# Deformable sampling: the running sums leave PSUM's chain of products and are added in SBUF by GpSimd

## The chip, the cores and the metric

The kernel runs on one core of a Trainium2 chip. The metric is the device time of one launch in microseconds (us). Shapes are written as partitions x elements per partition.

## What is computed

A block of convolution with attention: a deformable convolution (DCNv3) on a 4 x 56 x 56 x 128 image, an attention layer over all rows, and a mixture of experts. The change lies in the deformable sampling alone:

```python
B, H, W, C, G = (4, 56, 56, 128, 16); K = 9; GC = C // G
px = gx + dx + off[..., 0]
py = gy + dy + off[..., 1]
x0 = jnp.floor(pxf); y0 = jnp.floor(pyf)
for cx, cy in ((x0, y0), (x0 + 1, y0), (x0, y0 + 1), (x0 + 1, y0 + 1)):
    wgt = (1 - jnp.abs(pxf - cx)) * (1 - jnp.abs(pyf - cy))
    v = jnp.take_along_axis(xg, idx, axis=1)
    acc = acc + (wgt * valid)[..., None] * v
out = (acc * mf).reshape(B, H * W, K, G, GC).sum(axis=2)
```

Each pixel has 16 groups of 8 channels, and each group samples the projected image at 9 places of its own, bilinearly, with softmax weights over the 9.

## The kernel before

The program is a row of stages with a barrier of all engines between them: offsets and masks (about 80 to 700 us), a table of windows (to 741 us), the sampling (741 to 2215 us), the rest of the block over rows (to about 2515 us), attention, and the experts.

**The sampling stage** (`deformable_stage`, which calls `window_pass`) replaces the gather by arithmetic. The 128 partitions are 128 tiles of 7 x 14 pixels. The work is cut in 32 units: 16 channel groups (g) by two halves (v) of a tile, 49 pixels each. For a unit, every tap's bilinear weight is written as a product of two "hat" functions of row and column, and the weights of the nine taps are added into one grid `wd` of 8 x 8 shifts around each pixel. The unit's output is then the sum over these 64 shifts of weight times shifted image.

- SyncE loads the offsets (`om`) and the window of the image (`xw`) of the next group, 32 DMAs a group.
- ScalarE (`hats`, `clear`) computes the hat functions and zeroes `wd`, one unit ahead; `finish` (L714 to L720) moves a finished unit out of PSUM.
- VectorE (`build_step`) adds up the next unit's grid (L768, L774, L785, L792), and between these steps makes the current unit's products (`apply`, L832): 16 instructions of 4 shifts, 128x1568 elements, in a ring of four buffers `prod`.
- TensorE (L736 to L749) adds the products up in PSUM: an identity matrix times each 392-column quarter of a product, 64 matmuls a unit, into one of two accumulators `acc[:, v]`. In float32 each matmul is two records of the profile.
- GpSimd has nothing to do in this stage.

What has already been summed for these output elements lies in `y_all` (128 x 98 x 128 in SBUF, zeroed in an earlier stage at L252), since the pass can run for several windows of positions; with these inputs it runs once. Before a unit's products, one more matmul puts the old sums into the accumulator (L743), and `finish` copies the accumulator back over them (L717):

```python
pe.matmul(out, ident[:, :], unit_y(g, v), start=True, stop=False)      # L743
nc.scalar.activation(unit_y(g, v), acc[:, v, 0:UPX * GC]..., ACT.Copy)  # L717
```

`unit_y` (L676) is the unit's part of `y_all`: 7 rows of 7 pixels of 8 channels, 392 elements in runs of 8 with a step of 128. What orders the work: `prod_ok` and `prod_used` between VectorE and TensorE (VectorE is at most four products ahead), `acc_free` from `finish` to TensorE, `hats_ok` and `blank` from ScalarE to VectorE, `dstep` between VectorE's own steps. `hold` (L86) waits and then raises a semaphore of its own. After the pass GpSimd clears the semaphores (L886), and VectorE steps the window (L889 to L893).

Of the kernel before, what the change touches and what calls it, by code (L numbers as in the profile page):

```python
# [7 lines left out]
ALU = mybir.AluOpType  # L8
ACT = mybir.ActivationFunctionType
# [5 lines left out]
G, K = 16, 9  # L15
GC = C // G
# [11 lines left out]
R = 4  # L28
GRID = 8
OFFMAX = 58.0  # L30
LANES = 128
NB8, NXB = 8, 4
BY, BX = H // NB8, W // NXB
PX = BY * BX
UX = BX // 2
UPX = BY * UX
# [49 lines left out]
def hold(eng, sem, value, own):  # L86

    eng.wait_ge(sem, value)
    eng.sem_inc(own, 1)
# [508 lines left out]
NPROD = 4  # L598
# [37 lines left out]
def window_pass(nc, k, tb, bufs, sems, xg_d, om_d, y_all):  # L636

    own, ident = k["own"], k["ident"]
    om, xw, hat, mk, wd, prod, zeros, acc, ad = bufs
    (om_in, x_in, rel_ok, abs_ok, hats_ok, blank, hym_ok, dstep, prod_ok, prod_used, acc_free, y_ok) = sems  # L640
    DVE, SP = mybir.EngineType.DVE, mybir.EngineType.SP
    NCHUNK = 2 * GRID
    why = "an offset within the grid of positions, clamped when the table was made"
# [1 line left out]
    with nc.Block() as block:  # L645
# [30 lines left out]
        def unit_y(g, v):  # L676

            y = y_all[:, :, :].rearrange("p (y x) c -> p y x c", x=BX)
            return y[:, :, v * UX:(v + 1) * UX, bass.ds(g * GC, GC)]

        @block.scalar
        def _(act):
            act.sem_inc(acc_free, 2)

            def hats(g, v):
                n = g * 2 + v
                h = hat[:, v, :, :, :]
                if v == 0:
                    hold(act, om_in, g * 256 + 256, own)
                for s in range(2 * K):  # L690
                    d, tap = s // K, s % K
                    last = nc.scalar.activation(  # L692
                        h[:, s, R - 1, :].rearrange("p (y x) -> p y x", x=UX),
                        om[:, g % 2, :, v * UX:(v + 1) * UX, s], ACT.Identity,
                        bias=tb["nsk"][:, :, :, :].rearrange("p g d k -> p (g d k)")[:, bass.ds(g * (2 * K) + s, 1)],
                        scale=1.0)
                last.then_inc(rel_ok, 1)
                nc.scalar.activation(mk[:, v, :, :].rearrange("p k (y x) -> p k y x", x=UX),
                                     om[:, g % 2, :, v * UX:(v + 1) * UX, 2 * K:POS].rearrange("p y x k -> p k y x"),
                                     ACT.Copy)  # L700
                hold(act, rel_ok, n + 1, own)
                for r in range(R):
                    last = nc.scalar.activation(h[:, :, r, :], h[:, :, R - 1, :], ACT.Abs, bias=tb["negr"][:, r:r + 1],
                                                scale=1.0)
                last.then_inc(abs_ok, 1)
                hold(act, abs_ok, n + 1, own)
                flat = h.rearrange("p s r q -> p (s r q)")
                nc.scalar.activation(flat, flat, ACT.Relu, bias=1.0, scale=-1.0).then_inc(hats_ok, 1)

            def clear(v):  # L710
                nc.scalar.activation(wd[:, v, 0:GRID * WROW], zeros[:, 0:1].to_broadcast([LANES, GRID * WROW]), ACT.Copy)\  # L711
                    .then_inc(blank, 1)

            def finish(g, v):  # L714
                n = g * 2 + v
                hold(act, prod_used, n * NCHUNK + (NCHUNK + NPROD), own)
                nc.scalar.activation(unit_y(g, v), acc[:, v, 0:UPX * GC].rearrange("p (y x c) -> p y x c", y=BY, x=UX),  # L717
                                     ACT.Copy).then_inc(y_ok, 1)
                hold(act, y_ok, n + 1, own)
                act.sem_inc(acc_free, 1)  # L720

            for v in range(2):
                hats(0, v)
                clear(v)
            with act.Fori(0, G - 1) as g:
                for v in range(2):
                    n = g * 2 + v
                    hold(act, dstep, (n + 1) * PER, own)
                    hats(g + 1, v)
                    hold(act, prod_ok, (n + 1) * NCHUNK, own)  # L730
                    clear(v)
                    finish(g, v)
            for v in range(2):
                finish(G - 1, v)

        @block.tensor  # L736
        def _(pe):
            with pe.Fori(0, G) as g:
                for v in range(2):
                    n = g * 2 + v  # L740
                    hold(pe, acc_free, n + 1, own)
                    out = acc[:, v, 0:UPX * GC]
                    pe.matmul(out, ident[:, :], unit_y(g, v), start=True, stop=False)  # L743
                    for s in range(NCHUNK):
                        pe.wait_ge(prod_ok, n * NCHUNK + (s + 1))
                        for i in range(NXH):
                            mm = pe.matmul(out, ident[:, :], prod[:, s % NPROD, i, :], start=False,  # L747
                                           stop=(s == NCHUNK - 1 and i == NXH - 1))
                        mm.then_inc(prod_used, 1)  # L749

# [100 lines left out]
def deformable_stage(nc, k, tb, xg_d, om_d, y_all):  # L851

    with ExitStack() as es:
        t = Ctx(nc, es, "deform")
        names = ("om_loaded x_loaded rel_ready abs_ready hats_ready grid_blank hym_ready dve_step prod_ready prod_used "
                 "acc_free y_ready").split()
        sems = [t.sem(s) for s in names]
        tstep = t.sem("table_step")
        tmp = {"sr": t.sb("sr", [LANES, G, 2, K]), "wf": t.sb("wf", [1, G, K]), "pc": t.sb("pc", [1, G, 2]),
               "xf": t.sb("xf", [1, G])}  # L860
        zeros = t.sb("zeros", [LANES, 1])
        bufs = (t.sb("om", [LANES, 2, BY, BX, POS]), t.sb("xw", [LANES, 2, LANE_ROWS, LANE_COLS]),
                t.sb("hat", [LANES, 2, 2 * K, R, UPX]), t.sb("mk", [LANES, 2, K, UPX]),
                t.sb("wd", [LANES, 2, GRID * WROW + R * UPX]),
                t.sb("prod", [LANES, NPROD, NXH, UPX * GC]), zeros, t.ps("acc", [LANES, 2, 512]),
                t.sb("ad", [LANES, 4, R, R * UPX]))

        def move(body):
            with nc.Block() as block:
                @block.vector  # L870
                def _(dve):
                    body(dve)

        def restart(dve):
            nc.vector.memset(zeros[:, :], 0.0)
            nc.vector.tensor_copy(tb["p0"][:, :, :], tb["base"][:, :, :])

        move(restart)
        why = "a count of windows, bounded by the clamp of the offsets"
        nx, ny = (nc.values_load(tb["counts"][0:1, i:i + 1], min_val=1, max_val=int(2 * OFFMAX + 6) // R + 1,  # L880
                                 skip_runtime_bounds_check_because=why) for i in range(2))
        with nc.Fori(0, ny) as iy:
            with nc.Fori(0, nx) as ix:
                pass_tables(nc, tb, tmp, tstep)
                window_pass(nc, k, tb, bufs, sems, xg_d, om_d, y_all)
                for s in sems + [tstep, k["own"]]:  # L886
                    nc.gpsimd.sem_clear(s)
                nc.all_engine_barrier()
                move(lambda dve: nc.vector.tensor_scalar(tb["p0"][:, :, 0], tb["p0"][:, :, 0], tb["step"][:, 0:1], None,  # L889
                                                         ALU.add))  # L890
            move(lambda dve: nc.vector.tensor_scalar(tb["p0"][:, :, 1], tb["p0"][:, :, 1], tb["step"][:, 1:2], None,
                                                     ALU.add))
            move(lambda dve: nc.vector.tensor_copy(tb["p0"][:, :, 0], tb["base"][:, :, 0]))  # L893
# [1394 lines left out]
```

## Time and profile before

| | |
|---|---|
| median of 3 timed runs | 4370.42 us (4362.55, 4370.42, 4370.85) |
| the profiled execution: its time | 4365.95 us |
| the profiled execution: its span | 4364.2 us |
| TensorE busy, whole span | 3101.0 us (71%) |
| VectorE busy, whole span | 3029.8 us (69%) |
| ScalarE busy, whole span | 1418.7 us (33%) |
| GpSimd busy, whole span | 686.7 us (16%) |

The busy shares are means over stages that have different limits; what bounds the sampling is to be read from that stage. The time of an execution holds 1.75 us more than its span. In the profile PE is TensorE's matmuls, PEld its weight loads, DVE VectorE, ACT ScalarE, POOL GpSimd, SP SyncE; a q behind a name is that engine's instruction queue. Records of matmuls overlap, since they are pipelined: their pitch, from start to start, tells more than their length.

### The profile page before, as it was taken

To read this page: it belongs to the slowest core of one execution; us is meant where nothing else is said; L and a number is where in the kernel's file an instruction comes from. 1 tells how busy PE (TensorE), PEld (TensorE's weight loads), DVE (VectorE), ACT (ScalarE), POOL (GpSimd) and SP (SyncE) were. 2 spreads that over 40 slices of the span, in tenths; PEclk is the share of its full clock that TensorE was granted. 3 is DMA by queue.
4 is the path that set the end of the run, shared out by engine and by line. 5 is a ranking of instruction groups with operands and counts; after the bars stand their busy time and mean duration, and the time that the engine had idled before them with its cause. 6 is when DMAs were issued, how large, how long until landed. Compare 5 with 4: busy or idle time off the path is not lost. (4 is left out here: it accounts for less than half of the span.)

```text
span 4364.2 us, 40182 instructions
## 1 busy us (share of the span) xinstructions
PE 3101.0 (71%) x10947; PEld 1781.1 (41%) x10947; DVE 3029.8 (69%) x4442; ACT 1418.7 (33%) x2562; POOL 686.7 (16%) x724
## 2 busy tenths in 40 slices
PE   0144432799999999999965559999999996308940
PEld 0022221455555555555543324454544444306630
DVE  0387875899999999999969946666666664400026
ACT  0022221543333434242111145536455440103332
POOL 1033221000000000000035500111111111360036
PEclk9967666899999999999977679999999995559975
DMA  7732213222121212121021110010010102002223
GB/s 168 182 80 52 51 49 75 43 29 29 24 35 24 34 23 33 27 34 24 0 66 48 47 52 1 1 45 1 17 28 1 30 1 84 6 25 80 82 61 87
DMA packets 210585, 193.86 MB, mean 44 GB/s; under 512 B 65997, under 2 KB 181597, under 8 KB 210016
## 3 DMA queue, kind: packets, MB, share of 16 engines
q1 hardware_dynamic: 171506, 141.42, 15.3%
q10 hardware_dynamic: 32686, 42.09, 4.0%
q0 software_dynamic: 6272, 8.99, 1.1%
q8 instruction: 45, 0.74, 0.1%
q14 instruction: 76, 0.62, 0.0%
HBM read 94.01 MB, written 102.30 MB: 45 GB/s over the span
## 5 line engine op out<-in xcount | busy, mean ns | idle before, releaser
L747 PE MATMUL deform_acc<-deform_prod,all_ident 128*128 128x392 f32 x4096 | 1379.9, 495 | 74.3 <-DVE deform_prod L832 69.0
L747 PEld LDWEIGHTS deform_acc<-deform_prod,all_ident 128*128 128x128 f32 x4096 | 769.5, 190 | 680.1 <-DVE deform_prod L832 173.0
L832 DVE TENSOR_TENSOR deform_prod<-deform_xw,deform_wd 128x1568 f32<-128x1568 f32 x512 | 910.3, 1789 | 19.3 <-DVE deform_wd L792 10.8
L1494 PE MATMUL attn_ps_r<-attn_prob,attn_xs 128*128 128x448 f32 (+1 forms) x1400 | 607.6, 563 | 64.4 <-DVE attn_xr L1710 57.0
L1591 ACT ACTIVATE attn_prob<-attn_ps_e,attn_nm 128x896 f32<-128x896 f32 (+3 forms) x400 | 364.8, 913 | 469.8 <-DVE attn_nm L1679 467.9
L1679 DVE TENSOR_REDUCE attn_nm<-attn_ps_e 128x1 f32<-128x896 f32 (+3 forms) x400 | 385.4, 970 | 163.6 <-PE attn_ps_e L1482 152.7
L1494 PEld LDWEIGHTS attn_ps_r<-attn_prob,attn_xs 128*128 128x128 f32 (+1 forms) x1400 | 256.3, 194 | 313.7 <-issue 188.2
L711 ACT ACTIVATE deform_wd<-deform_zeros 128x3136 f32<-128x3136 f32 x32 | 90.1, 2815 | 805.9 <-DVE deform_prod L832 805.9
L2141 DVE TENSOR_TENSOR experts_yo<-experts_ps_y,experts_b 128x512 f32<-128x512 f32 x32 | 22.1, 691 | 394.3 <-PE experts_ps_y L2081 394.3
L1710 DVE TENSOR_TENSOR attn_xr<-attn_xr,attn_ps_r 128x448 f32<-128x448 f32 x252 | 155.7, 618 | 160.1 <-PE attn_ps_r L1494 157.5
L792 DVE TENSOR_TENSOR deform_wd<-deform_wd,deform_ad 128x784 f32 x256 | 249.4, 974 | 1.0 <-DVE deform_wd L792 0.5
L985 POOL MEMSET rows_half<- 128x4 f32 x1 | 0.1, 101 | 1519.5 <-POOLq L67 1519.5
L1391 POOL TENSOR_TENSOR attn_xs<-attn_xa,attn_wz 128x508 f32<-128x508 f32 (+1 forms) x100 | 100.7, 1032 | 863.1 <-DVE attn_wz L1700 863.1
L785 DVE TENSOR_TENSOR deform_ad<-deform_hat 128x1568 f32<-128x1568 f32 x128 | 228.8, 1788 | 0.0
L1482 PE MATMUL attn_ps_e<-attn_ka,attn_qa 128*128 128x448 bf16 (+1 forms) x700 | 200.9, 357 | 9.4 <-DVE attn_qb L1672 5.6
L1482 PE MATMUL attn_ps_e<-attn_kb,attn_qb 128*128 128x448 bf16 (+1 forms) x700 | 200.0, 356 | 0.0
L692 ACT ACTIVATE deform_hat<-deform_om,block_nsk 128x49 f32 (+1 forms) x576 | 162.8, 375 | 97.4 <-DMA deform_om<-offsets_masks 74.4
L301 PE MATMUL offs_ps_x<-all_ident,offs_x_sb 112*128 112x112 f32 x112 | 26.1, 385 | 193.9 <-ACT offs_xt L356 181.8
L292 PE MATMUL offs_ps_c<-all_ident,offs_conv 128*112 128x128 f32 x112 | 21.4, 324 | 190.6 <-DVEq L468 129.0
L2111 ACT ACTIVATE experts_hid<-experts_ps_u,experts_b1t 128x512 f32<-128x512 f32 x128 | 87.8, 687 | 163.7 <-PE experts_ps_u L2070 163.6
L2081 PE MATMUL experts_ps_y<-experts_w,experts_hid 128*128 128x128 f32 x1024 | 121.9, 277 | 23.0 <-ACT experts_hid L2111 23.0
L460 DVE TENSOR_SCALAR offs_conv<-offs_xpad,block_w_dw,block_b_dw_col 128x1568 f32<-128x1568 f32 x8 | 8.4, 1092 | 184.3 <-ACT offs_xt L356 184.3
(299 smaller groups left out, 4118.4 us busy)
## 6 DMA issues: line engine op xcount, KB each, us to landing
offsets_masks<-offs_om SPq DMA_DIRECT2D x56, 378.0 KB
deform_om<-offsets_masks SPq DMA_DIRECT2D x256, 82.7 KB
deform_xw<-projected SPq DMA_DIRECT2D x256, 73.5 KB
projected<-offs_zero ACTq DMA_DIRECT2D x1, 17000.0 KB
dispatched<-offs_zero ACTq DMA_DIRECT2D x1, 8192.0 KB
experts_bi<-dispatched SPq DMA_DIRECT2D x32, 256.0 KB, 3.3
expert_out<-experts_yo ACTq DMA_DIRECT2D x32, 256.0 KB, 3.8
projected<-offs_zero ACTq DMA_DIRECT2D x1, 7480.0 KB
```

The lines of the kernel that those rows point to most:

```text
L692: last = nc.scalar.activation(h[:, s, R - 1, :].rearrange("p (y x) -> p y x", x=UX), om[:, g % 2, :, v * UX:(v + 1) * UX, s], ACT.Identity ...
L747: mm = pe.matmul(out, ident[:, :], prod[:, s % NPROD, i, :], start=False, stop=(s == NCHUNK - 1 and i == NXH - 1))
L785: nc.vector.tensor_tensor(dst, spread(hat[:, v, tap:tap + 2, :, :], 2, R), spread(hat[:, v, K + tap:K + tap + 2, :, :], 3, R), ALU.mult).t ...
L792: nc.vector.tensor_tensor(region, region, temp(tap), ALU.add).then_inc(dstep, 1)
L832: nc.vector.tensor_tensor(prod[:, s % NPROD, :, :].rearrange("p d (y x c) -> p d y x c", y=BY, x=UX), x, spread(w.rearrange("p (d y x) -> ...
L1391: pool.tensor_tensor(xs[0:rows, at + i, :, 0:C - 1], spread(xa[0:rows, b % 2, tile, 0:C - 1], 1, NCH), spread(wz[0:rows, e, i, :], 2, C - ...
L1482: mm = pe.matmul(ps_e[u % NE][0:rows, hf, 0:BK], q_[:, S % 2, at:at + rows], k_[:, b % 2, m0:m0 + BK], start=q_ is qa, stop=q_ is qb)
L1494: mm = pe.matmul(ps_r[:, 0:BK], xs[0:rows, at + i, j // 2, :], prob[0:rows, at + i, j * BK:(j + 1) * BK], start=(i == 0), stop=(i == len(t ...
L1591: nc.scalar.activation(prob[0:rows, slab(S) + i, m0:m0 + n * BK].rearrange("p (a f) -> p a f", a=n), ps_e[u % NE][0:rows, 0:n, 0:BK], ACT. ...
L1679: nc.vector.tensor_reduce(nm[0:rows, S % 2, i, ch:ch + 1], ps_e[u % NE][0:rows, 0:halves(ch), 0:BK], mybir.AxisListType.XY, ALU.max, negat ...
L1710: nc.vector.tensor_tensor(part, part, ps_r[:, 0:BK], ALU.add).then_inc(r_ok, 1)
L2081: mm = pe.matmul(ps_y[p][:, j * C:(j + 1) * C], hid[:, p, f, j * 128:(j + 1) * 128], w2[:, x, f, :], start=(f == 0), stop=(f == FB - 1))
```

## The change

The matmul that puts the old sums into the accumulator is gone; the first product's matmul starts the accumulator instead. `finish` copies the accumulator to a new buffer `sums` (128 x 2 x 392, one part for each half v), and GpSimd, with a block of its own in the pass, adds that buffer to the unit's part of `y_all`, in place. A new semaphore `added` tells ScalarE that the half's buffer may be written again; it starts at 2. One more semaphore is cleared at the end of the pass.

```diff
         @block.scalar
         def _(act):
-            act.sem_inc(acc_free, 2)
-
...
             def finish(g, v):
                 n = g * 2 + v
                 hold(act, prod_used, n * NCHUNK + (NCHUNK + NPROD), own)
-                nc.scalar.activation(unit_y(g, v), acc[:, v, 0:UPX * GC].rearrange("p (y x c) -> p y x c", y=BY, x=UX),
-                                     ACT.Copy).then_inc(y_ok, 1)
+                hold(act, added, n + 1, own)
+                nc.scalar.activation(sums[:, v, :], acc[:, v, 0:UPX * GC], ACT.Copy).then_inc(y_ok, 1)
                 hold(act, y_ok, n + 1, own)
                 act.sem_inc(acc_free, 1)
 
+            act.sem_inc(acc_free, 2)
...
+        @block.gpsimd
+        def _(pool):
+            pool.sem_inc(added, 2)
+            with pool.Fori(0, G) as g:
+                for v in range(2):
+                    n = g * 2 + v
+                    hold(pool, y_ok, n + 1, own)
+                    part = unit_y(g, v)
+                    pool.tensor_tensor(part, part, sums[:, v, :].rearrange("p (y x c) -> p y x c", y=BY, x=UX),
+                                       ALU.add).then_inc(added, 1)
+
         @block.tensor
...
                     out = acc[:, v, 0:UPX * GC]
-                    pe.matmul(out, ident[:, :], unit_y(g, v), start=True, stop=False)
                     for s in range(NCHUNK):
                         pe.wait_ge(prod_ok, n * NCHUNK + (s + 1))
                         for i in range(NXH):
-                            mm = pe.matmul(out, ident[:, :], prod[:, s % NPROD, i, :], start=False,
+                            mm = pe.matmul(out, ident[:, :], prod[:, s % NPROD, i, :], start=(s == 0 and i == 0),
                                            stop=(s == NCHUNK - 1 and i == NXH - 1))
```

## Rows read from the trace of the kernel before

**Rows 1.** The page, part 2: tenths of busy time in 40 slices of 109 us

```profile
DVE  0387875899999999999969946666666664400026
POOL 1033221000000000000035500111111111360036
```

**Rows 2.** Windows, 800 to 2160 us: stretch, length, busy us (instructions), PEclk, DMA, GB/s

```profile
800.00:2160.00 1360.00, 1337.25 (x3993) 748.54 (x3992) 1349.09 (x921) 483.83 (x773) 0.00 (x0) 1.00 0.20 27
```

**Rows 3.** Waits, 800 to 2160 us: us in total, times, longest

```profile
PEld deform_acc L747 <- DVE deform_prod L832: 119.1, 236, 1.1
PE deform_acc L747 <- DVE deform_prod L832: 17.6, 44, 0.5
DVE deform_prod L832 <- DVE deform_wd L792: 10.4, 28, 0.4
DVE deform_prod L832 <- PE deform_acc L747: 0.3, 1, 0.3
```

**Rows 4.** Timeline, from the first product to a unit's border: start, us, work

```profile
792.69 3.49 DVE L832 TENSOR_TENSOR deform_prod<-deform_xw,deform_wd 128x1568 f32<-128x1568 f32 x2 [0.39 <-DVE deform_wd L792]
...
1193.37 0.52 PEld L743 LDWEIGHTS deform_acc<-block_y_all,all_ident 128*128 128x128 f32 x2
1194.08 0.50 ACT L717 ACTIVATE block_y_all<-deform_acc 128x392 f32 x1 [0.32 <-PE deform_acc L747]
1195.45 1.99 DVE L768 TENSOR_TENSOR deform_hat<-deform_hat,deform_mk 128x1764 f32<-128x1764 f32 x1
1197.36 1.78 DVE L832 TENSOR_TENSOR deform_prod<-deform_xw,deform_wd 128x1568 f32<-128x1568 f32 x1
```

**Rows 5.** Timeline, the last unit and the end of the stage

```profile
2167.84 10.30 DVE L832 TENSOR_TENSOR deform_prod<-deform_xw,deform_wd 128x1568 f32<-128x1568 f32 x6
2169.69 0.82 PE L743 MATMUL deform_acc<-block_y_all,all_ident 128*128 x2
2170.34 42.30 PE L747 MATMUL deform_acc<-deform_prod,all_ident 128*128 128x392 f32 x128
2178.45 1.79 DVE L832 TENSOR_TENSOR deform_prod<-deform_xw,deform_wd 128x1568 f32<-128x1568 f32 x1 [0.30 <-PE deform_acc L747]
2212.77 0.50 ACT L717 ACTIVATE block_y_all<-deform_acc 128x392 f32<-128x392 f32 x1 [42.30 <-PE deform_acc L747]
2214.97 0.23 DVE L889 TENSOR_SCALAR block_p<-block_p,block_step 128x16 f32<-128x16 f32 x1 [11.03 <-PEq L888]
```

**Rows 6.** Groups by form, GpSimd: xcount, busy us, mean ns, idle before

```profile
L1391 POOL TENSOR_TENSOR attn_xs<-attn_xa,attn_wz 128x508 f32<-128x508 f32 x96 | 96.8, 1032 | 863.1 <-DVE attn_wz L1700 863.1
L268 POOL TENSOR_TENSOR offs_om<-offs_om,offs_mx x28 | 33.5, 1196 | 43.1 <-DVE offs_mx L449 42.6
L1402 POOL TENSOR_TENSOR attn_tin<-attn_tin,attn_xa 128x512 f32<-128x512 f32 x24 | 30.3, 1266 | 120.2 <-DMA attn_tin<-block_out 120.2
L1402 POOL TENSOR_TENSOR attn_tin<-attn_tin,attn_xa 64x128 f32<-64x128 f32 x4 | 1.8, 447 | 1.0 <-DMA attn_tin<-block_out 1.0
```

**Rows 7.** Timeline of DVE and POOL in the rows stage; last row: L1095's min/median/max ns

```profile
2246.80 0.69 DVE L1101 TENSOR_TENSOR rows_z<-rows_z,rows_gg 128x512 f32<-128x512 f32 x1
2246.92 1.69 POOL L994 TENSOR_TENSOR rows_x_all<-rows_x_all,rows_gb 128x512 f32<-128x512 f32 x1
2247.41 1.79 DVE L1095 TENSOR_SCALAR rows_z<-rows_z,rows_mv,rows_rs 128x128 f32<-128x128 f32 x3
...
L1095 DVE TENSOR_SCALAR rows_z<-rows_z,rows_mv,rows_rs x196: 302/334/1295, 2230.9 to 2508.1; 128x128 f32<-128x128 f32 x196
```

**Rows 8.** Timeline of DVE and POOL, offsets stage, two places; last row: L259's min/median/max ns

```profile
234.46 1.36 DVE L438 SCALAR_TENSOR_TENSOR first_extremes<-offs_om,first_extremes 112x1152 f32<-112x1152 f32 x1
234.61 1.29 POOL L259 TENSOR_SCALAR offs_ve<-offs_mv 112x4 f32<-112x4 f32 x1 [0.47 <-DVE offs_mv L400]
...
278.28 1.32 POOL L274 TENSOR_TENSOR offs_om<-offs_om,offs_mx  x1 [4.36 <-DVE offs_mx L428]
278.90 1.92 DVE L438 SCALAR_TENSOR_TENSOR first_extremes<-offs_om,first_extremes 112x1152 f32<-112x1152 f32 x1 [0.34 <-DVE offs_om L430]
...
L259 POOL TENSOR_SCALAR offs_ve<-offs_mv x28: 222/1298/1316, 206.4 to 671.3; 112x4 f32<-112x4 f32 x28
```

More of the change, by code:

```diff
@@ L638, in window_pass @@
     own, ident = k["own"], k["ident"]
-    om, xw, hat, mk, wd, prod, zeros, acc, ad = bufs
-    (om_in, x_in, rel_ok, abs_ok, hats_ok, blank, hym_ok, dstep, prod_ok, prod_used, acc_free, y_ok) = sems
+    om, xw, hat, mk, wd, prod, zeros, acc, ad, sums = bufs
+    (om_in, x_in, rel_ok, abs_ok, hats_ok, blank, hym_ok, dstep, prod_ok, prod_used, acc_free, y_ok, added) = sems
     DVE, SP = mybir.EngineType.DVE, mybir.EngineType.SP
@@ L855, in deformable_stage @@
         names = ("om_loaded x_loaded rel_ready abs_ready hats_ready grid_blank hym_ready dve_step prod_ready prod_used "
-                 "acc_free y_ready").split()
+                 "acc_free y_ready added").split()
         sems = [t.sem(s) for s in names]
@@ L865, in deformable_stage @@
                 t.sb("prod", [LANES, NPROD, NXH, UPX * GC]), zeros, t.ps("acc", [LANES, 2, 512]),
-                t.sb("ad", [LANES, 4, R, R * UPX]))
+                t.sb("ad", [LANES, 4, R, R * UPX]), t.sb("sums", [LANES, 2, UPX * GC]))
         def move(body):
```

## The prediction

> **What bounds the kernel now.** I read the slices of the page first, then the windows, the waits and the timeline of the one stage that the change touches. The slices show VectorE at nine tenths or more from about 800 to 2160 us, with GpSimd at zero [rows 1]. In that stretch of 1360 us VectorE is busy 1349.1 us (99.2%), TensorE 1337.3 us, at a granted clock of 1.00 throughout [rows 2]. Both look full, and the waits tell them apart: TensorE and its weight loads wait for VectorE's products again and again (119.1 us in 236 waits, 17.6 us in 44), while VectorE waited for TensorE once, for 0.3 us. What is left of VectorE's idle time is a step of its own, 0.4 us at the head of a unit [rows 3]. So the sampling goes at VectorE's pace. From the first product of unit 0 (792.69) to that of unit 31 (2167.84) are 31 units, 44.36 us each [rows 4, 5]. Only the last unit is different: VectorE has no next grid to build, it waits for free buffers from 2178.45 on, and TensorE sets the end: 128 records in 42.30 us, a pitch of 0.33 us [rows 5].
>
> **What the change removes.** One float32 matmul a unit (L743), two records, which take TensorE 0.65 us from start to the next unit's first product matmul (2169.69 to 2170.34) [rows 5]. Over 32 units that is 21 us of TensorE's time. In the units 0 to 30 it buys nothing, because TensorE then only waits longer for VectorE, whose waits for it sum to 0.3 us [rows 3]. In the last unit it is on the path: **-0.65 us**.
>
> **What it adds on ScalarE.** The same copy of 392 elements (0.50 us, L717 [rows 4]), now to contiguous SBUF, and one more wait, for the add of two units earlier, some 88 us back. Nothing: ScalarE is busy 483.8 of the 1360 us [rows 2], and TensorE gets its accumulator back a unit early. If that wait ever did hold, the hats of a later unit would be queued behind it, and VectorE would wait for them.
>
> **What it adds on GpSimd: 32 adds.** First their length. Two inputs that are both full, as here, took 1266 ns for 512 elements and 447 ns for 128 [rows 6]: 2.13 ns an element and 0.17 us beside it, so 392 elements are **1.01 us**. Where one input repeats along the inner run it is cheaper, 1032 ns for 508 and 1196 ns for 576 elements [rows 6], which scaled to 392 is 0.80 us: my low end. L268 works on runs of 9 elements of 27 and is not slow; runs of 8 with a step of 128, as in `y_all`, no row shows.
>
> **What an add does to VectorE.** This is the term that decides, and GpSimd's idleness hides nothing of it, since VectorE has no gap of 1 us in the stage. Two places of the trace show the two engines getting into each other's way, in both directions:
>
> - GpSimd waits for VectorE. L259 works on 4 elements a partition and takes 222 ns at best, but 1.3 us when it starts beside L438, which has two inputs in SBUF: it ends at 235.90, just after L438 (235.82) [rows 8]. In the rows stage L994, an add of 512 elements like L1402, takes 1.69 us instead of 1.27 since L1101 is under way at its start [rows 7].
> - Then VectorE waits for GpSimd. The first L1095 behind L1101 takes up to 1295 ns instead of the median 334, because L994 runs till 2248.61: **0.96 us lost to an add of 1.27 us** [rows 7]. And L438, with two SBUF inputs like every VectorE instruction of the sampling (products, grid steps, mask), took 1.92 instead of 1.36 us where L274 still had 0.70 us to run: 0.56 us lost [rows 8].
>
> Both also show that the waiting GpSimd instruction gets in at the end of the VectorE instruction that held it, ahead of VectorE's next one. In the sampling stage VectorE runs one after another without a gap, so each add starts beside a product or a mask step (at 1194.6 it would be a product, with L768 next [rows 4]), waits for its end, and delays the next one. The size, from an add of 1.01 us: by L1095 the loss is the add's length less 0.31 us, 0.70 us. By L438, 0.14 us of what remained was no loss, another 0.14 us of GpSimd's record lies ahead of its need (L259 ends 0.08 us after L438 though it lasts 0.22 alone), and consecutive VectorE records overlap by 0.09 us, which is given up too: 1.01 - 0.28 + 0.09 = 0.82 us. I take the mean, **0.76 us**. The low end is the cheap add by the first rule, 0.80 - 0.31 = 0.49 us; the high end for a normal add 0.82 us.
>
> How often: the add of unit n falls at the head of unit n+1. For n = 0 to 29 that unit is bound by VectorE: 30 x 0.76 = **+22.8 us** (30 x 0.49 = 14.7 to 30 x 0.82 = 24.6). TensorE does not soften it; it only idles longer. The add of unit 30 falls into the last unit, where VectorE later idles for TensorE [rows 5]: nothing.
>
> The Trainium skill speaks against the change more sharply: "SBUF — State Buffer", section "Who interferes with whom", says that a VectorE instruction with two SBUF inputs and a GpSimd instruction that reads SBUF exclude each other for the whole instruction, whoever comes first. With a whole instruction lost each time the sum would be 30 x 1.01 = 30.3 us; the rows show the exclusion, but a loss some 0.2 to 0.3 us shorter, and I go by them.
>
> **The end of the stage.** The last add has no cover. Before, ScalarE's last copy ended at 2213.27 and the step of the window came at 2214.97 [rows 5]; now GpSimd's 1.01 us and some 0.2 us of semaphores lie between: **+1.2 us**. One semaphore more to clear: under 0.1 us, inside this. The other stages are the same.
>
> **Sum.** -0.65 + 22.8 + 1.2 = **+23.4 us** on the profiled execution's 4365.95 us, 4389.4. That execution is 4.5 us below the median shown; the four times of this kernel average 4367.4. I set the forecast between the sums on both, at **4391 us**.
>
> **The rivals.** A measurement of this kernel can tell 0.2% from no change, 8.7 us.
>
> - *No price (same).* GpSimd never gets in between VectorE's back-to-back instructions, or reads in VectorE's gaps (0.4 us at the head of a unit [rows 3]), and has 88 us for its 1 us. For it: in rows 7 the instruction that was overtaken has one tensor input, and the one overtaken behind L259 lost next to nothing to so small an operation. Against it: L438 itself lost 0.56 us. Time: 4366 to 4371 plus 0.55, about **4369**. Chance 0.11.
> - *Slow add (slower by more).* The 8-element runs of `y_all`, read and written, cost GpSimd twice the time, 2.0 us. Loss 2.0 - 0.25 = 1.75 us a unit, 30 times: +52 us, **4420**. Against it: L268's runs of 9 [rows 6]. Chance 0.07.
> - *TensorE is the bound (faster).* Place: the head of each unit, where it works off a backlog of products with L743 in front. If the 98% of rows 2 were a real limit, the removed 0.65 us would shorten each of 32 units: -21 us, **4347**, provided that the adds cost VectorE less than that. It decides only from the point at which VectorE waits for free product buffers; rows 3 have one such wait of 0.3 us. Chance 0.05.
>
> **How the numbers follow.** The forecast's case has the rest, 0.77. Its own ends are 14.7 + 0.55 on 4365.95, which is 4381, and 24.6 + 0.55 on 4370.4, which is 4396. To leave out no more than 2 in 10, the range takes in a somewhat slower add (1.3 us, a loss of about 1.0 us, +31) and 2 us of spread below: **4379 to 4402**. Slower by over 0.2%: 0.77 + 0.07, less the edge of the low end, 0.83; within 0.2%: 0.12; faster: 0.05.
>
> **What would show it.** In the profile after: VectorE's records no longer have the same length; once a unit a product or mask step (L768, L832) is 0.7 to 0.8 us longer than its 1.99 or 1.79 us; the pitch of the units is 45.1 instead of 44.36 us. GpSimd's adds last 1.0 us plus the wait for the instruction under way, up to 2.7 us, and 1.0 us for the last. VectorE's busy share stays at 99%, as the loss lies inside its records; TensorE's waits for products grow by about 1.4 us a unit. At the end L889 follows ScalarE's last copy by 2.9 instead of 1.7 us. I am wrong if the pitch stays at 44.4 (no exclusion between these forms), if an uncovered add lasts 2 us, or if TensorE's granted clock falls below 1.00 with its added idle time.

## The result, and the profile after

The changed kernel takes **4395.21 us** (median of 5, 4389.88 to 4401.05) where the kernel before takes 4370.42 us (median of 5, 4362.55 to 4375.50). The ratio is 1.0058, with a 95% interval of 1.0046 to 1.0071: slower by 0.6%, 24.8 us between the medians. The forecast was 4391 us, with 4379 to 4402 as its range. The profiled execution took 4389.88 us, with a span of 4388.1 us, 23.9 us more than before.

The same views as before, of the changed kernel. First the slices of the page and the windows view of 800 to 2160 us (busy us of PE, PEld, DVE, ACT, POOL, then PEclk, the DMA's share and GB/s):

```profile
DVE  0387874999999999999969946666666664400026
POOL 1033221000000000000025501010111111360036
...
800.00:2160.00 1360.00, 1309.20 (x3859) 717.56 (x3858) 1349.10 (x904) 484.38 (x775) 47.75 (x30) 1.00 0.20 27
```

VectorE's busy time is the same to a hundredth of a per cent, 1349.1 us, but it holds 904 instructions instead of 921 [rows 2]. A busy share says nothing of work done. GpSimd's 30 adds do not show in the slices at all: 47.75 us in 1360 is less than a tenth. TensorE's granted clock is 1.00 in this stretch, as before. The waits of the same stretch:

```profile
PEld deform_acc L756 <- DVE deform_prod L841: 192.2, 321, 1.2
PE deform_acc L756 <- DVE deform_prod L841: 45.9, 88, 0.6
DVE deform_prod L841 <- DVE deform_wd L801: 10.8, 29, 0.4
```

TensorE waits longer for VectorE (119.1 and 17.6 us before [rows 3]), and VectorE no longer waits for TensorE here at all. So the bound is what it was, and has become slower. Where, shows the view of single lines (min/median/max ns, first and last start in us); GpSimd's add is now L743, the mask step L777, the product L841:

```profile
L743 POOL TENSOR_TENSOR block_y_all<-block_y_all,deform_sums x32: 1001/1590/1660, 842.3 to 2240.0; 128x392 f32 x32
L777 DVE TENSOR_TENSOR deform_hat<-deform_hat,deform_mk x32: 1987/2810/2831, 774.8 to 2153.2; 128x1764 f32<-128x1764 f32 x32
L841 DVE TENSOR_TENSOR deform_prod<-deform_xw,deform_wd x512: 1772/1778/2606, 794.8 to 2228.5; 128x1568 f32<-128x1568 f32 x171
```

The mask step took 1.99 us in every unit; now it takes 2.80 to 2.83 us in the 30 units in front of which an add falls (median of all 32: 2.81). No other VectorE instruction of the sampling became longer, but for one product of the last unit (2606 ns). The timeline at one border between units shows how it comes about:

```profile
1202.82 0.50 ACT L716 ACTIVATE deform_sums<-deform_acc 128x392 f32<-128x392 f32 x1 [0.32 <-PE deform_acc L756]
1203.58 1.58 POOL L743 TENSOR_TENSOR block_y_all<-block_y_all,deform_sums 128x392 f32 x1 [43.59 <-ACT deform_sums L716]
1204.19 2.82 DVE L777 TENSOR_TENSOR deform_hat<-deform_hat,deform_mk 128x1764 f32<-128x1764 f32 x1
```

The add starts while a product is under way, waits for its end (about 1204.28, since records overlap by 0.09 us), works until 1205.16, and the mask step behind the product ends 0.83 us late. ScalarE's copy comes at the same point of every unit, so in this kernel it is always the mask step that pays. And the end of the stage (last unit's first products, last copy, last add, step of the window):

```profile
794.81 3.49 DVE L841 TENSOR_TENSOR deform_prod<-deform_xw,deform_wd 128x1568 f32<-128x1568 f32 x2 [0.39 <-DVE deform_wd L801]
...
2194.79 14.53 DVE L841 TENSOR_TENSOR deform_prod<-deform_xw,deform_wd 128x1568 f32<-128x1568 f32 x8
2197.78 1.38 POOL L743 TENSOR_TENSOR block_y_all<-block_y_all,deform_sums 128x392 f32 x1 [43.60 <-ACT deform_sums L716]
2239.25 0.50 ACT L716 ACTIVATE deform_sums<-deform_acc 128x392 f32<-128x392 f32 x1 [41.74 <-PE deform_acc L756]
2240.01 1.00 POOL L743 TENSOR_TENSOR block_y_all<-block_y_all,deform_sums 128x392 f32 x1 [40.85 <-ACT deform_sums L716]
2242.67 0.23 DVE L898 TENSOR_SCALAR block_p<-block_p,block_step 128x16 f32<-128x16 f32 x1 [12.34 <-PEq L897]
```

From unit 0's first product to unit 31's are now 1399.98 us, before 1375.15 [rows 4, 5]: +24.8. From there to the step of the window are 47.88 us, before 47.13: +0.75. Together 25.6 us. The span grew by less than that, 23.9 us; the difference lies in stages that the change does not touch: unit 0's first product comes 2.1 us later, and what follows the sampling is 3.8 us shorter. In the experiments below the first product lies anywhere from 794 to 800 us, also where nothing ahead of it differs from the kernel before, so such differences are from run to run. Below I therefore read the **pitch of the units** (first product to first product, mean over the 28 units from unit 1 on): 44.375 us before, 45.204 after.

### The profile page after: what moved, and what is told of

Read it like the earlier page. It is cut to its first block and busy times, and to the rows that moved or that the text cites. A ratio compares the mean times of both kernels' runs of the same rounds, so it can differ in the third digit from the quotient of the medians.

```text
span 4388.1 us, 40187 instructions
## 1 busy us (share of the span) xinstructions
PE 3085.1 (70%) x10883; PEld 1756.7 (40%) x10883; DVE 3055.9 (70%) x4442; ACT 1419.4 (32%) x2562; POOL 736.6 (17%) x756
## 5 line engine op out<-in xcount | busy, mean ns | idle before, releaser
L841 DVE TENSOR_TENSOR deform_prod<-deform_xw,deform_wd 128x1568 f32<-128x1568 f32 x512 | 906.3, 1781 | 18.1 <-DVE deform_wd L801 11.2
L743 POOL TENSOR_TENSOR block_y_all<-block_y_all,deform_sums 128x392 f32 x32 | 50.1, 1567 | 1494.7 <-ACT deform_sums L716 1494.7
```

Source lines behind the costliest of these rows:

```text
L841: nc.vector.tensor_tensor(prod[:, s % NPROD, :, :].rearrange("p d (y x c) -> p d y x c", y=BY, x=UX), x, spread(w.rearrange("p (d y x) -> ...
```

## The experiments

Theory 1: GpSimd's add and a VectorE instruction with two inputs in SBUF exclude each other while they read; the removed matmul was worth nothing outside the last unit. The rivals are named in each expectation. Reference times of the kernel before on the same chips: medians 4368.65 to 4369.26 us (13 runs each); the changed kernel was not timed again beside them. Where an experiment has one run, its time says little, since runs of one kernel lie up to 18 us apart, and the argument rests on the pitch and on the records of its trace. The edits are shown against the changed kernel, except in "No add at all" and "The add on VectorE", which start from the kernel before; `...` stands for lines left out.

**No add at all.** The kernel before, less the matmul:

```diff
-                    pe.matmul(out, ident[:, :], unit_y(g, v), start=True, stop=False)
...
-                            mm = pe.matmul(out, ident[:, :], prod[:, s % NPROD, i, :], start=False,
+                            mm = pe.matmul(out, ident[:, :], prod[:, s % NPROD, i, :], start=(s == 0 and i == 0),
```

> The kernel before without the matmul that reads the old sums into PSUM, and with no add at all: ScalarE writes each finished unit straight over its part of y_all. It leaves out the summing over several windows. Theory 1 (the add and VectorE exclude each other; the matmul was free): the pitch of the units stays at 44.36 us as before, and only the last unit is shorter, by 0.65 us, so the time is that of the kernel before within its spread. Rival (TensorE is a real limit of each unit): the pitch falls by up to 0.65 us a unit, 20 us in all.

Measured: 4370.19 us against 4368.65, ratio 1.000 (0.9990 to 1.0009). The pitch is 44.378 us. Its last unit, by its first products and the step of the window:

```profile
2175.58 12.00 DVE L831 TENSOR_TENSOR deform_prod<-deform_xw,deform_wd 128x1568 f32<-128x1568 f32 x7
2219.96 0.50 ACT L717 ACTIVATE block_y_all<-deform_acc 128x392 f32<-128x392 f32 x1 [41.74 <-PE deform_acc L746]
2222.16 0.23 DVE L888 TENSOR_SCALAR block_p<-block_p,block_step 128x16 f32<-128x16 f32 x1 [11.03 <-PEq L887]
```

46.58 us instead of 47.13, so 0.55 us gained, once. TensorE was no limit of the other units, though it is busy for 98% of the stretch in the kernel before.

**Matmul and add together.**

```diff
+                    pe.matmul(out, ident[:, :], unit_y(g, v), start=True, stop=False)
...
-                            mm = pe.matmul(out, ident[:, :], prod[:, s % NPROD, i, :], start=(s == 0 and i == 0),
+                            mm = pe.matmul(out, ident[:, :], prod[:, s % NPROD, i, :], start=False,
```

> The changed kernel with the removed matmul put back, so that both the matmul and GpSimd's add are there (it counts old sums twice where there are several windows). Theory 1: the pitch is that of the changed kernel, 45.2 us, since TensorE still waits for VectorE, and the stage is longer by 0.65 us in the last unit alone. Rival (the matmul's removal gave back part of the add's price): the pitch goes above 45.2, towards 45.9 us.

Measured: 4400.79 us (one run), a pitch of 45.209 us, and 48.44 us for the last unit, 0.56 more than the changed kernel's. The two parts of the change are independent: the matmul is worth 0.55 us in the last unit and nothing else, whether the add is there or not.

**A fill in place of the add.**

```diff
...
-                nc.scalar.activation(sums[:, v, :], acc[:, v, 0:UPX * GC], ACT.Copy).then_inc(y_ok, 1)
+                nc.scalar.activation(unit_y(g, v), acc[:, v, 0:UPX * GC].rearrange("p (y x c) -> p y x c", y=BY, x=UX),
+                                     ACT.Copy).then_inc(y_ok, 1)
...
-                    part = unit_y(g, v)
-                    pool.tensor_tensor(part, part, sums[:, v, :].rearrange("p (y x c) -> p y x c", y=BY, x=UX),
-                                       ALU.add).then_inc(added, 1)
+                    pool.memset(spare[:, v, :], 0.0).then_inc(added, 1)
```

> No matmul, ScalarE writes the unit straight over y_all as in the run without an add, and GpSimd, at the place where the add stood, fills 1024 elements a partition of a spare buffer with zero; it leaves out the summing over windows. The fill only writes SBUF and should last about 0.9 us by the fills of the trace of before, about as long as the add. Theory 1, in the form that what is shared is a read of SBUF: the mask step L777 stays at 1.99 us, the pitch at 44.4 us, and the fill itself takes no longer beside VectorE. Rival (any GpSimd instruction of such a length holds VectorE up): the mask step takes 2.7 us and the pitch is 45.1 us.

Its lines (min/median/max ns), and the timeline at a border:

```profile
L743 POOL MEMSET deform_spare<- x32: 951/951/952, 842.3 to 2214.8; 128x1024 f32 x32
L776 DVE TENSOR_TENSOR deform_hat<-deform_hat,deform_mk x32: 1987/1990/1997, 774.5 to 2129.0; 128x1764 f32<-128x1764 f32 x32
...
1196.61 0.95 POOL L743 MEMSET deform_spare<- 128x1024 f32 x1 [43.47 <-ACT block_y_all L716]
1197.26 1.99 DVE L776 TENSOR_TENSOR deform_hat<-deform_hat,deform_mk 128x1764 f32<-128x1764 f32 x1
```

The fill starts beside a product like the add did, and neither waits for the other: 951 ns every time, the mask step at 1.99, the pitch at 44.378 us. It is not GpSimd's work as such, nor its writes. (4357.43 us, one run; what follows the sampling was 11 us shorter in it than in the profile of the kernel before.)

**Four of seven rows.**

```diff
-                    part = unit_y(g, v)
-                    pool.tensor_tensor(part, part, sums[:, v, :].rearrange("p (y x c) -> p y x c", y=BY, x=UX),
+                    part = unit_y(g, v)[:, 0:4, :, :]
+                    pool.tensor_tensor(part, part,
+                                       sums[:, v, 0:4 * UX * GC].rearrange("p (y x c) -> p y x c", y=4, x=UX),
```

> The changed kernel with GpSimd adding only 4 of the 7 rows of pixels of a unit, 224 elements instead of 392; the other three rows are left out. Theory 1, loss = length of the add less about 0.19 us: the add takes 0.17 + 224 x 2.13 ns = 0.65 us uncovered, the mask step is 0.46 us longer than 1.99 instead of 0.82, the pitch is 44.83 us. Rival (a fixed price for each handover between the engines): the mask step stays at 2.8 us and the pitch at 45.2 us.

```profile
L743 POOL TENSOR_TENSOR block_y_all<-block_y_all,deform_sums x32: 649/1228/1978, 846.2 to 2232.3; 128x224 f32 x32
L778 DVE TENSOR_TENSOR deform_hat<-deform_hat,deform_mk x32: 1991/2453/2466, 777.9 to 2145.9; 128x1764 f32<-128x1764 f32 x32
...
845.65 1.99 DVE L778 TENSOR_TENSOR deform_hat<-deform_hat,deform_mk 128x1764 f32<-128x1764 f32 x1
846.19 1.98 POOL L743 TENSOR_TENSOR block_y_all<-block_y_all,deform_sums 128x224 f32 x1 [145.62 <-ACT deform_sums L716]
847.55 2.27 DVE L842 TENSOR_TENSOR deform_prod<-deform_xw,deform_wd 128x1568 f32<-128x1568 f32 x1
```

The add alone takes 649 ns (the minimum, as in the uncovered last unit), the mask step 0.46 us more than before, the pitch is 44.845 us. The loss follows the length; it is no fixed price for a handover. 4377.72 us, one run. The three timeline rows are of the first add, the only one here that starts beside the mask step and not beside the product in front of it. It waits the mask step out, and the product behind pays, 2.27 instead of 1.78 us: what counts is which instruction comes next, not that it is the mask step. The copy and the dense add below have one such first unit too.

**Two adds in a row.**

```diff
...
-                                       ALU.add).then_inc(added, 1)
+                                       ALU.add)
+                    pool.tensor_tensor(spare[:, v, :], sums[:, v, :], sums[:, v, :], ALU.add).then_inc(added, 1)
```

> The changed kernel with a second add of 392 elements behind the first one, from the buffer of the finished unit to a spare buffer, so each unit has two GpSimd adds in a row. Theory 1 with the waiting instruction getting in at each border: VectorE's blocked instruction runs once the first add is done, the second add waits for its end and then holds up the next one, so two VectorE instructions a unit lose 0.82 us each and the pitch is 44.37 + 1.64 = 46.0 us. Variant (GpSimd keeps the port between its two instructions): one VectorE instruction loses about 1.9 us and the pitch is 46.2 to 46.3 us. Rival (one loss a unit whatever GpSimd does, the second add finding a gap): 45.2 us.

The timelines of GpSimd and VectorE at one border, and the second add's line:

```profile
1029.65 1.56 POOL L743 TENSOR_TENSOR block_y_all<-block_y_all,deform_sums 128x392 f32 x1 [41.69 <-ACT deform_sums L716]
1031.18 2.59 POOL L745 TENSOR_TENSOR deform_spare<-deform_sums 128x392 f32<-128x392 f32 x1
...
1030.27 2.80 DVE L778 TENSOR_TENSOR deform_hat<-deform_hat,deform_mk 128x1764 f32<-128x1764 f32 x1
1032.99 2.42 DVE L842 TENSOR_TENSOR deform_prod<-deform_xw,deform_wd 128x1568 f32<-128x1568 f32 x1
...
L745 POOL TENSOR_TENSOR deform_spare<-deform_sums x32: 839/2592/2623, 847.8 to 2264.7; 128x392 f32<-128x392 f32 x32
```

The engines take turns: the mask step gets in between the two adds, the second add waits for it (its record lasts 2.59 us) and then holds up the next product, 2.42 instead of 1.78 us. The pitch is 45.851 us, +1.476, and not +1.64, because the second add is shorter, 839 ns alone: 0.82 + 0.64 = 1.46. 4414.48 us, one run. That an add of the same 392 elements was shorter is taken up below.

**The add on VectorE.** The matmul goes, ScalarE's copy too, and VectorE adds a finished unit from PSUM behind the sixth product of the next one:

```diff
+            def finish(g, v):
+                n = g * 2 + v
+                hold(dve, prod_used, n * NCHUNK + (NCHUNK + NPROD), own)
+                part = unit_y(g, v)
+                nc.vector.tensor_tensor(part, part, acc[:, v, 0:UPX * GC].rearrange("p (y x c) -> p y x c", y=BY, x=UX),
+                                        ALU.add).then_inc(acc_free, 1)
...
+                    if s == 5 and done is not None:
+                        finish(*done)
```

> No matmul and no GpSimd add: VectorE adds the finished unit from PSUM to its part of y_all, after the sixth product of the next unit, and ScalarE's copy is gone. It does all the work of the reference. A 448-element add with one input in PSUM took 0.62 us in the trace of before, so one of 392 should take about 0.56 us, of which 0.09 us overlaps its neighbour: the pitch rises by 0.47 us to 44.83 us, 31 units give +14.6 us, less the last unit's matmul, with the last add at the end in place of ScalarE's copy. Expected about 14 us above the kernel before and 10 us below the changed one. Rival (the add in VectorE's stream costs as much as GpSimd's, for instance because it waits for TensorE): 45.2 us or more.

```profile
L813 DVE TENSOR_TENSOR block_y_all<-block_y_all,deform_acc x32: 553/556/565, 860.3 to 2233.5; 128x392 f32 x28, 128x392 f32<-128x392 f32 x4
```

Measured: 4381.30 us against 4369.26, ratio 1.0025 (1.0015 to 1.0035), 12.0 us between the medians where about 14 were expected; the pitch is 44.855 us, +0.48. So the bound engine does the addition itself for 0.48 us a unit, where "offloading" it costs the same engine 0.83 us.

**The masks in PSUM.** The changed kernel with one operand moved:

```diff
-                t.sb("hat", [LANES, 2, 2 * K, R, UPX]), t.sb("mk", [LANES, 2, K, UPX]),
+                t.sb("hat", [LANES, 2, 2 * K, R, UPX]), t.ps("mk", [LANES, 2, 512])[:, :, 0:K * UPX].rearrange("p v (k q) -> p v k q", q=UPX),
```

> The changed kernel with one buffer moved: the softmax masks mk lie in PSUM instead of SBUF, so the mask step L777, which is the instruction that the add always held up, reads one input from SBUF and one from PSUM. It does all the work of the reference. Theory 1 (the exclusion is about the second SBUF input of VectorE): the add still waits for the product in front of it, then runs beside the mask step, which stays near 2.0 us; the pitch is back at 44.4 us and the time within 2 us of the kernel before, about 23 us below the changed one. Rival (a GpSimd add holds up any VectorE instruction): the mask step stays at 2.8 us, the pitch at 45.2 us.

```profile
L743 POOL TENSOR_TENSOR block_y_all<-block_y_all,deform_sums x32: 999/1598/1663, 846.1 to 2219.0; 128x392 f32 x32
L777 DVE TENSOR_TENSOR deform_hat<-deform_hat,deform_mk x32: 1983/1985/1993, 778.6 to 2133.0; 128x1764 f32<-128x1764 f32 x32
...
1200.75 1.60 POOL L743 TENSOR_TENSOR block_y_all<-block_y_all,deform_sums 128x392 f32 x1 [42.74 <-ACT deform_sums L716]
1201.37 1.99 DVE L777 TENSOR_TENSOR deform_hat<-deform_hat,deform_mk 128x1764 f32<-128x1764 f32 x1
```

The add still waits for the product (median 1598 ns, like 1590 in the changed kernel), then runs beside the mask step without touching it. The pitch is 44.376 us, and the time 4365.55 us against 4368.68 of the kernel before: ratio 1.000 (0.9986 to 1.0013). The whole loss of 0.83 us a unit is gone. What is left is the longer end of the stage, 47.88 us from unit 31 to the step of the window, as in the changed kernel. This is the run that settles the cause for the mask step: the same two instructions at the same place, and only the memory of one VectorE operand differs.

**A copy in place of the add.**

```diff
-                    pool.tensor_tensor(part, part, sums[:, v, :].rearrange("p (y x c) -> p y x c", y=BY, x=UX),
-                                       ALU.add).then_inc(added, 1)
+                    pool.tensor_copy(part, sums[:, v, :].rearrange("p (y x c) -> p y x c", y=BY, x=UX)).then_inc(added, 1)
```

> The changed kernel with GpSimd copying the finished unit over its part of y_all instead of adding, so it has one SBUF input of 392 elements; it leaves out the summing over windows. Theory 1 (any reading GpSimd instruction excludes VectorE's two-input ones, for its uncovered length less 0.19 us): whatever the copy lasts uncovered in the last unit, the mask step is longer than 1.99 us by that less 0.19; by the GpSimd rows of before I expect 0.4 to 0.7 us uncovered, so a pitch of 44.6 to 44.9 us. Rival (only a two-input add excludes): the pitch is 44.38 us.

```profile
L743 POOL COPY block_y_all<-deform_sums x32: 513/1092/2097, 843.7 to 2225.6; 128x392 f32 x32
L776 DVE TENSOR_TENSOR deform_hat<-deform_hat,deform_mk x32: 1990/2301/2305, 775.7 to 2139.3; 128x1764 f32<-128x1764 f32 x32
```

One input is enough: the copy lasts 0.51 us alone and costs the mask step 0.31 us, the pitch is 44.693 us, the time 4372.32 us (one run).

**A dense add of two different buffers.** No matmul, ScalarE writes the unit over `y_all`, and GpSimd adds two spare buffers in the add's place:

```diff
...
-                    part = unit_y(g, v)
-                    pool.tensor_tensor(part, part, sums[:, v, :].rearrange("p (y x c) -> p y x c", y=BY, x=UX),
-                                       ALU.add).then_inc(added, 1)
+                    pool.tensor_tensor(spare[:, v, :], xa[:, v, :], xb[:, v, :], ALU.add).then_inc(added, 1)
```

> ScalarE writes the unit straight over y_all; GpSimd adds two different spare buffers into a third, all dense, 392 elements, at the place of the add. It leaves out the summing over windows. It asks why the second add of the run with two adds lasted only 0.84 us uncovered. If dense runs are cheaper than the 8-element runs of y_all: 0.84 us here too, mask step + 0.65, pitch 45.03. If it was cheap because both its inputs were the same buffer: 1.00 us, mask step + 0.82, pitch 45.2 us.

```profile
L743 POOL TENSOR_TENSOR deform_spare<-deform_xa,deform_xb x32: 1008/1598/2829, 846.5 to 2244.3; 128x392 f32<-128x392 f32 x32
L776 DVE TENSOR_TENSOR deform_hat<-deform_hat,deform_mk x32: 1990/2829/2836, 779.0 to 2157.6; 128x1764 f32<-128x1764 f32 x32
```

1008 ns and +0.84 us on the mask step, pitch 45.220 us (4392.85 us, one run). The 8-element runs of `y_all` cost GpSimd nothing; it is the add with the same buffer as both its inputs that is shorter. That the short one also was the second of two in a row does not explain it by the rows there are: in the kernel before, the 512-element adds of L1402 that follow another GpSimd instruction at once take 1.26 us at least, and so do those behind a pause.

Over these runs GpSimd's length alone and VectorE's loss go together: 0.51 and 0.31, 0.65 and 0.46, 0.84 and 0.64, 1.00 and 0.82, 1.01 and 0.84 us. The loss is the length less 0.17 to 0.20 us.

## Why the prediction was right

**What bounds.** Right, and the clock stayed at 1.00. The rival with TensorE as the bound needed 0.65 us from each unit and is refuted by the run without an add, at a pitch of 44.378 us. The one wait of 0.3 us [rows 3] had said so, against a busy share of 98%.

**The matmul, -0.65 us.** It measured -0.55 us, once; 0.56 when put back. By the starts of TensorE's records the first product matmul of the last unit did come 0.65 us earlier, 1.85 us behind the start of the first product (2.50 before [rows 5]), but its second record then came 0.43 us later and not 0.33, so 0.10 us was given back. Why, no run shows.

**The add's length, 1.01 us.** 1.00 us. The two-point line through the adds with full inputs [rows 6] was the one to use; the cheaper rows with a repeated input were the wrong kin. The slow add is refuted too: short strided runs made no difference.

**The loss, 0.76 us a unit.** This term was mis-sized: 0.83 us of pitch. I had averaged two places of the trace, and the one with VectorE's two-input instruction (L438 [rows 8], which gave 0.82 us) was right to a hundredth, though worked out from a single record. L1095 [rows 7] has a single tensor input, another form than any VectorE instruction of the sampling, and should have been left out; why it lost 0.1 us less no run shows. 30 x 0.83 = 24.9 us instead of 22.8, which is also just above the high end that I gave a normal add, 24.6. "A product or mask step" was too cautious: it is the mask step in all 30 units. The loss fell where a product ended and the mask step came next, as the prediction read off the border [rows 4].

**Thirty times, not 32.** Right. The add behind unit 30 made a product of the last unit 0.82 us longer (the 2606 ns), and it cost nothing, since VectorE waits for TensorE there: ScalarE's last copy comes 44.46 us after the unit's first product with this add and with the fill alike.

**The end, +1.2 us.** Against the run without an add, 46.58 us from unit 31 to the step of the window became 47.88: +1.30 us. The step came 2.92 us after ScalarE's last copy, as forecast (2.9), where it was 1.70: +1.22. The other 0.08 us lies in front of that copy (44.46 against 44.38 us from the first product), between TensorE's last matmul and ScalarE's start, in every run in which ScalarE has the additional wait for GpSimd. The prediction had put this wait at nothing.

**Sum.** -0.55 + 24.9 + 1.3 = 25.6 us in the sampling, where the forecast had 23.4. The median came out 4 us above the forecast: 2.2 us from these terms, the rest within the spread of the executions. That it lies 1 us inside the end of the forecast's own case (4396) is luck of that spread, since the terms came out above it.

**The rival without a price** is refuted by the changed kernel itself. Its argument was that GpSimd might never get in; the run with two adds shows them taking turns. The Trainium skill's rule for this pair ("SBUF — State Buffer", section "Who interferes with whom": a VectorE instruction with two SBUF inputs contends with a GpSimd instruction that reads SBUF, not with one that only writes it) is borne out: the fill cost nothing and the copy 0.31 us, the mask step with one input in PSUM lost nothing, and wherever both conditions held the later one waited. Only "for the whole instruction", which the page says of this pair in its section "🔬 SBUF: two separate sides", is some 0.2 us too much here, as the rows before had said.

**What stays open.** Two inputs in SBUF are not shown to be the only form that can be held up: L1095 [rows 7] lost 0.96 us with a single tensor input, and no run here takes that apart. Nor does a run move an operand of a product (`prod`, L832) or of a grid step to PSUM.

**What was off.** TensorE's longer waits: forecast 1.4 us a unit, but the weight loads' waits grew by 73 us in the stretch (192.2 from 119.1), some 2.4 us a unit, while TensorE's busy time fell by 28 us, 0.9 a unit. How a wait is split between the two queues I have not taken apart; it has no effect on the time.

## What to carry to other kernels

GpSimd is not a free helper beside a VectorE that works on pairs of SBUF tensors without a gap: each of its instructions that reads SBUF (0.5 to 1.0 us long in these runs) took its own length, less some 0.2 us, from VectorE, so work moved there pays only where it would cost VectorE more than that (here the addition itself costs VectorE 0.48 us and the help 0.83). Before moving such work, find the VectorE instruction that will stand next to it and ask whether one of its operands can lie in PSUM. And take work off an engine only if another one waits for it: a busy share of 98% hid that the removed matmuls were worth 0.55 us in the whole kernel.

## What the hardware showed that I had not expected

Moving one operand of one VectorE instruction to PSUM took the whole 0.83 us a unit away and cost that instruction nothing (1985 ns against 1990). I had not thought of it when I predicted.

A GpSimd add whose two inputs are the same buffer took 839 ns for 392 elements; with two different buffers it took 1008 ns, as dense as the other. Why, no run here shows.

No version here beats the kernel before by more than can be measured: the masks in PSUM and the run without an add (which leaves out the summing over windows) both stand at a ratio of 1.000 to it.
